# Two of the four high parts of the feed-forward's inner layer moved from VectorE to ScalarE, and the last group's z turned by TensorE

## The reference

```python
tgt1 = _layer_norm(tgt, g1, be1)
tgt = tgt + _self_attn(tgt1, mask, Wq, bq, Wk, bk, Wv, bv, Wo, bo)
tgt = tgt + (memory @ Wg.T + bg)
tgt1 = _layer_norm(tgt, g2, be2)
ff = jax.nn.relu(tgt1 @ W1.T + b1) @ W2.T + b2
return tgt + ff
```

## Time and profile before

| | us |
|---|---|
| median of three runs (lowest, highest) | 1756.54 (1755.94, 1760.69) |
| the profiled execution, its own time | 1759.22 |
| span of its trace | 1757.3 |
| mean granted clock of TensorE, as a share | 0.99 |
| busy: PE, DVE, ACT, POOL | 1684.2, 1509.3, 1393.1, 953.5 |

### The profile page before, as it was taken

One profiled execution on the slowest core, in us unless ns is written; L12 is line 12 of the kernel. 1 busy time (PEld: TensorE's weight loads), 2 busy tenths in 40 slices (PEclk: granted clock), 3 DMA queues, 4 the chain that ended last, 5 costly groups with the idle time before them and its releaser, 6 DMA issues. The chain is left out here.

```text
span 1757.3 us, 53486 instructions
## 1 busy us (share of the span) xinstructions
PE 1684.2 (96%) x17272; PEld 1643.0 (93%) x17272; DVE 1509.3 (86%) x7136; ACT 1393.1 (79%) x5506; POOL 953.5 (54%) x906
## 2 busy tenths in 40 slices
PE   6799999999999999999999999999999999999997
PEld 5699999999999999999999999999999999999997
DVE  7798898898888888888888888888888888888873
ACT  4788788788788788788788788788788787787782
POOL 5355545545545545555555555555555555555544
PEclk8899999999999999999999999999999999999999
DMA  5434444444444444444444444444444444444421
GB/s 187 130 124 138 140 131 138 131 139 132 134 142 130 137 140 130 136 141 131 136 145 128 136 142 131 135 142 132 134 139 136 133 141 135 128 146 135 128 91 37
DMA packets 258951, 233.77 MB, mean 133 GB/s; under 512 B 26992, under 2 KB 209136, under 8 KB 258672
## 3 DMA queue, kind: packets, MB, share of 16 engines
q1 hardware_dynamic: 258672, 230.35, 41.5%
HBM read 62.73 MB, written 16.78 MB: 45 GB/s over the span
## 5 line engine op out<-in xcount | busy, mean ns | idle before, releaser
L448 ACT ACTIVATE scores<-scores,row_min 128x128 f32<-128x128 f32 x2048 | 799.5, 406 | 37.1 <-DVE row_min L725 37.1
L874 POOL TENSOR_TENSOR hT_lo<-hid,hT_hi 128x512 fp32r<-128x512 f32 x256 | 339.6, 1327 | 687.7 <-DVE hT_hi L684 687.7
L725 DVE CUSTOM_DVE_ANT_0 scores<-score_ps,mask_bias 128x128 f32<-128x128 f32 x2048 | 467.8, 286 | 1.5 <-issue 1.1
L448 ACT ACTIVATION_READ_ACCUMULATOR scores<-scores,row_min 128x1 f32 x2048 | 420.5, 205 | 0.0
L460 ACT ACTIVATE probs<-turn_ps 128x512 f32<-128x512 f32 x512 | 306.3, 599 | 92.6 <-PE turn_ps L1022 92.6
L956 PE MATMUL ffn_ps<-w_hi,hT_lo 128*128 128x256 f32 x1024 | 301.2, 294 | 32.6 <-POOL hT_lo L874 32.2
L1022 PE MATMUL turn_ps<-ident,scores 128*128 128x128 f32 x2048 | 307.1, 273 | 5.3 <-ACT probs L460 5.3
L956 PE MATMUL ffn_ps<-zT_hi,w_lo 128*128 128x256 f32 x992 | 294.0, 296 | 1.4 <-ACT hid L501 1.2
L958 PE MATMUL ffn_ps<-w_hi,hT_hi 128*128 128x256 f32 x1024 | 284.2, 277 | 0.0
L957 PE MATMUL ffn_ps<-w_lo,hT_hi 128*128 128x256 f32 x1024 | 283.5, 277 | 0.0
L957 PE MATMUL ffn_ps<-zT_lo,w_hi 128*128 128x256 f32 x992 | 276.1, 278 | 0.0
(11 more groups left out here) (144 smaller groups left out, 4288.0 us busy)
## 6 DMA issues: line engine op xcount, KB each, us to landing
q_stack<-q_hi SPq DMA_DIRECT2D x128, 256.0 KB, 2.4
k_stack<-k_hi SPq DMA_DIRECT2D x256, 128.0 KB, 2.3
x_in<-x_dram SPq DMA_DIRECT2D x64, 256.0 KB, 2.7
mem_in<-memory_dram SPq DMA_DIRECT2D x64, 256.0 KB, 3.0
x_res<-x_dram SPq DMA_DIRECT2D x64, 256.0 KB, 3.0
q_stack<-q_lo SPq DMA_DIRECT2D x64, 256.0 KB, 2.3
k_stack<-k_lo SPq DMA_DIRECT2D x128, 128.0 KB, 2.3
inv<-inv_cols SPq DMA_DIRECT2D x256, 64.0 KB, 2.4
```

The costliest lines, as they stand in the source:

```text
L448: last = act.activation(exps, exps, ACT.Exp, bias=row_min[:, k, h:h + 1], scale=-1.0, accum_out=row_sum[:, k, h:h + 1])
L725: last = dve.tensor_tensor_reduce(out=scores[:, slot(i, t), h, :], in0=score_ps[t % 2][:, h * S:(h + 1) * S], in1=mask_bias[:, b, :], scal ...
L874: pool.tensor_tensor(halves[1], src, halves[0], ALU.subtract).then_inc(done, 1)
```

## The change

ACT now makes the high parts of the third and the fourth pair: right behind the two relu instructions of pair 2, and of pair 3, it waits for them and copies `hid` to `hT_hi`. DVE keeps the first two pairs. The new semaphore `hid_late_hi` tells POOL of the two that ACT makes, so each of the two semaphores counts two a group. In stage 64, for the last group only, DVE's turning in blocks and SP's four copies are gone: PE turns `xhat` with four transposes into a PSUM bank ahead of part 3 of the product with W2, ACT takes z's high part from that bank, and DVE the low part.

```diff
@@ ScalarE
                         last.then_inc(hid_relu, 1)
+                        if n >= 2:
+                            act.wait_ge(hid_relu, HJ * g + n + 1)
+                            act.activation(hT[0][:, 2 * n:2 * n + 2, :], hid[:, n % 2], ACT.Copy
+                                           ).then_inc(hid_late_hi, 1)
...
-                    if out_ and t == 12:
+                    if is_at(i, GROUPS) and t == 12:
+                        split_high(by_tile[1], zT[0][:], z_turned, 1, hid_ready, HJ * (GROUPS - 1), z_hi)
+                    elif out_ and t == 12:
@@ VectorE
-                    if ffn and t == 0:
+                    if is_at(i, GROUPS + 1) and t == 0:
+                        split_low(by_tile[1], zT, z_hi, GROUPS, z_split)
+                    elif ffn and t == 0:
...
-                    if ffn and t in HIDDEN_TICKS and t < 8:
+                    if ffn and t in HIDDEN_TICKS[:2]:
                         hidden_high(i - 2, HIDDEN_TICKS.index(t))
...
-                        dve.wait_ge(attnT_split, g + 1)
-                        turn_quads(attn_blocks, xhat2, ln2_ready, g + 1, z_blocked)
-                    if ffn and t == HIDDEN_TICKS[-1]:
-                        hidden_high(i - 2, HJ - 1)
+                        if i < GROUPS:
+                            dve.wait_ge(attnT_split, g + 1)
+                            turn_quads(attn_blocks, xhat2, ln2_ready, g + 1, z_blocked)
@@ GpSimd
-                        split_low(hid[:, n % 2], [h[:, 2 * n:2 * n + 2, :] for h in hT], hid_hi,
-                                  HJ * g + n + 1, hid_split)
+                        split_low(hid[:, n % 2], [h[:, 2 * n:2 * n + 2, :] for h in hT],
+                                  hid_hi if n < 2 else hid_late_hi, 2 * g + n % 2 + 1, hid_split)
@@ TensorE
+                    if is_at(i, GROUPS) and t == 12:
+                        pe.wait_ge(ln2_ready, GROUPS)
+                        pe.wait_ge(resid_ready, GROUPS)
+                        turn(by_tile[1], xhat2).then_inc(z_turned, 1)
@@ SyncE
-                if out_:
+                if out_ and i < GROUPS:
                     sp.wait_ge(z_blocked, i)
```

More of the change, by code:

```diff
@@ L226, in xattn_block @@
             sem(f"ln2_{n}") for n in ("stats", "mean", "var", "rstd", "ready"))
+        z_turned = sem("z_turned")
         z_blocked, z_cols, z_hi, z_split = (sem(f"z_{n}") for n in ("blocked", "cols", "hi", "split"))
         hid_ready, hid_relu, hid_hi, hid_split = (sem(f"s_hid_{n}") for n in ("ready", "relu", "hi", "split"))
+        hid_late_hi = sem("s_hid_late_hi")
         down_ready, resid_biased, y_summed = sem("down_ready"), sem("resid_biased"), sem("y_summed")
```

## The result

Before: 1757.43 us median (1755.94 to 1760.69, four runs; the 1756.54 of the table above was the median of three of them). After: **1823.55 us** (1806.31 to 1830.59, four runs). The recorded ratio, which weighs all runs, is 1.036, with a 95% interval of 1.028 to 1.044 (the two medians alone give 1.038): slower, and within the predicted 1762 to 1842 us, 6 us above the 1817.5. The profiled execution took 1826.82 us, with a span of 1825.0.

The account below looks back on a forecast made before the run. PE was taken to set the pace, 96% busy, with a second chain through DVE's norm and `values_of` almost as long. 1756.5 + 64 (61 stages at + 1.05) - 3 (last group) = 1817.5 us; range 1762 to 1842.

Parts of the forecast that it names:

- The sum of a stage: Per stage: DVE's chain + 1.86 - 0.27 us, less 0.54 slack, gives + 1.05 us; + 64 us over 61 stages.
- the slack of 0.54: Between ACT's copy of the probabilities and PE's `values_of`: 0.54 us a stage, beyond which delays lengthen the stage one for one.
- the two turns: POOL's low part of pair 3, then `xT_hi`, stop DVE's second norm, delaying it 1.86 us; chance 0.48.
- The loop: DVE's second norm and turning, z's copies, ACT's probabilities, PE's `values_of` and next fourth score matmul, back to DVE: 25.83 us.
- the first rival: Only one POOL instruction stops the second norm: + 0.21 us a stage, 1767 us, or 1773 with small delays; chance 0.27.
- some 1.5 us: PE's new wait each stage for ACT's copy of the probabilities ahead of `values_of`, replacing its wait for `hT_lo`.
- ACT's copies at nothing: ACT's two added copies, 1.4 us a stage, fall into its idle times and cost nothing; bounds 0 and 0.7 us.
- DVE's cast at 0.27: Removing DVE's cast at 813.07, ahead of the second norm, shortens DVE's chain by 0.27 us a stage.
- the last group at 3 us: Turning z on PE starts its product 2 us earlier and may avoid a 1.3 us clock loss: - 3 us once.
- Faster: the port doesn't matter: POOL's low part of pair 3 doesn't stop the second norm; 30 us gained, 1726 us; chance 0.15.
- PE's clock falls: PE's clock drops behind about 1.5 us idle each stage, adding 1.3 us a stage, about 1900 us; chance 0.03.
- The wait for `hT_lo`: PE's wait for POOL's low part: at most 32.2 us over 61 stages to gain, leaving PE alone at 25.84 a stage.

Follow-up runs that it names:

- 2: The changed kernel, with POOL's `xT_hi` also waiting until DVE has ended the second norm: 1782.80 us, ratio to before 1.012 to 1.015.
- 8: The changed kernel with only pair 3's high part on ACT, pair 2's back on DVE: 1842.49 us, ratio to before 1.047 to 1.051.
- 7: The changed kernel with only pair 2's high part on ACT, pair 3's back on DVE: 1738.04 us, ratio to before 0.986 to 0.989.
- 1: The changed kernel, with POOL's low part of pair 3 also waiting until the second norm has ended: 1724.55 us, ratio to before 0.979 to 0.982.
- 3: The kernel before, plus two unread copies of `hid` on ACT behind the relus of pairs 2 and 3: 1758.18 us, ratio 0.999 to 1.001.
- 4: The kernel before with only the last group's z turned by PE, as in the change: 1755.79 us, ratio 0.997 to 0.999.
- 9: The changed kernel, with POOL's low parts of pairs 1 and 3 waiting for the first and second norm: 1706.04 us, ratio to before 0.968 to 0.971.
- 10: The kernel before, with only POOL's low part of pair 1 waiting until the first norm has ended: 1712.17 us, ratio 0.972 to 0.975.
- 5: The kernel before, plus one unread addition on DVE ahead of the second norm: 1780.86 us, ratio 1.010 to 1.014.
- 12: The kernel before, with pair 3's cast to `hT_hi` and two unread DVE additions between second norm and turning: 1819.12 us, ratio 1.032 to 1.036.

## Why the prediction was right

**The sum of a stage.** "Chain: + 1.86 - 0.27" and "less the slack of 0.54: + 1.05 us" forecast a stage of 26.37 + 1.05 = 27.42 us; 27.42 and 27.44 stand in the trace. The norm's delay came out at 1.73 (2.61 - 0.88) and not 1.86, since the two turns follow each other closer than I had them, and 0.14 us came on top: 25.83 - 0.27 + 1.73 is 27.29, and the stage is 27.43. 2 and 8 show the same 0.14 and 0.17 us (8 without the - 0.27), so it isn't chance. The traces tell what it is. The loop is 25.88 by medians and not 25.83 (0.05), in part because PE follows the copy of `probs` by 0.10 us and not by the 0.06 that I took from another pair of engines. And DVE's way from `attn` to the norm is shorter by 0.21 and not by 0.27 (0.06). The last 0.03 is within what medians of parts leave over. The second of these is the small delay "of ACT's `k_hi`" that the first rival named with "up to 0.1 a stage". ACT's `k_hi` and DVE's `k_lo`, which waits for it, in a stage of the kernel before and in one of the kernel after:

```profile
805.36 0.84 ACT L515 ACTIVATE k_hi<-work_ps,qk_bias 128x256 fp32r<-128x256 f32 x2
806.68 0.84 DVE L788 SCALAR_TENSOR_TENSOR k_lo<-work_ps,qk_bias,k_hi 128x256 fp32r<-128x256 f32 x2
```

```profile
998.95 0.86 ACT L521 ACTIVATE k_hi<-work_ps,qk_bias 128x256 fp32r<-128x256 f32 x2
999.84 0.88 DVE L798 SCALAR_TENSOR_TENSOR k_lo<-work_ps,qk_bias,k_hi 128x256 fp32r<-128x256 f32 x2
```

Before, `k_hi` had ended 0.48 us before `k_lo` began (806.20 to 806.68); after, 0.03 (999.81 to 999.84), in most stages. For once the loop sets the pace, `values_of` starts 0.10 us behind ACT's copy where it started 0.62 behind, so ACT's program runs half a microsecond later beside PE's: `k_hi` starts 7.86 us behind the start of `values_of` in place of 7.34. In 7, where the loop doesn't set the pace, the same way of DVE is shorter by 0.32 us, so the cast was worth a little more than its 0.27, and the wait for `k_hi` costs about 0.1. In 1 the sum doesn't apply, since in most of its stages `values_of` doesn't wait for the copy. That the sum of a stage is right to 0.01 us is luck: the turns were 0.13 too long, and the rest 0.14 was missing. Its mechanism, the two turns and the loop, is what the traces show.

Of PE's wait I said "some 1.5 us" ahead of `values_of`. It is 1.09 in the median stage; the other part of PE's idle time stands in waits like the one for `hid` on the weight loads, 23.9 us in all.

**Two turns against one.** I gave 0.48 and 0.27, for "tenths". Both happen: two turns in about fifty stages, one in eleven. The first condition, POOL starting ahead of DVE, holds in both; the second, `xT_hi` ready in time, fails in the eleven. The Trainium skill ("SBUF — State Buffer", section "Who interferes with whom") has the rule for one turn, and the trace of 2 agrees, with 1.82 us in place of 0.88. What makes the loss of 66 us out of 25 is the second turn, which is beyond the rule.

**ACT's copies at nothing, DVE's cast at 0.27, the last group at 3 us.** Shown by 3 (0 us), by 8 against after (0.30 a stage), and by 4 (3.0 us, between 1.6 and 4.6 by its interval). In the last group the idle time goes from 1.23 + 2.74 to 1.38 us, the transposes take 0.60, so about 2 us are left as I had them, and the clock doesn't fall behind the 1.38. The 1.3 us for the clock are not safe: in the trace of 4 it fell a little earlier, as said above.

**The rivals.** "Faster: the port doesn't matter" fell at its own condition: the norm isn't left alone. But its mechanism stands: 1 fulfils the condition by a wait, and gives 1724.55 where the rival said 1726. "PE's clock falls" was put as all or nothing. It happens in four stages, in which a late landing has lengthened the wait to 1.96 to 2.44 us, less than the 2.74 on which the rival was built.

**The terms that were off.**
- *The wait for `hT_lo`.* I took 32.2 us / 61 = 0.53 from the rows of the matmuls, so PE alone at 25.84. It is 25.60 in 9 and 10, where nothing stops it: the wait cost 0.80 a stage. The row that shows it was in the same view, on the weight loads:

```profile
PEld ffn_ps L956 <- POOL hT_lo L874: 46.6, 61, 1.4
```

  46.6 / 61 = 0.76. The wait stood on the loads, and the matmul's own idle time leaves out the load that follows the wait. It left the sum as it is, since PE's own stage didn't decide, but it made the gain that was to be had look two thirds as large as it is (32.2 us, where 61 x 0.80 is 49), and the two limits look equal, where PE's is 25.60 and the loop's 25.88.
- *Late landings* had no term. Before, one landing is late, by 1.31 us (5.35 in place of 4.04), and its stage is 0.77 longer than 26.40: 1.31 less the slack of 0.54, to the hundredth. After the change the loop *is* the stage and there is no slack left: eight landings late by 0.85 to 1.6 us come through, with the clock in four: 15 us. The profiled execution took 1826.82 us, 6.8 above its forecast of 1820. Late landings and clock, less the 7.8 of the stages with one turn, are 7 to 8 us and account for that; the small delays beside them and the 3 us that the kernel before has of the same kind nearly cancel.
- *Where the slack applies.* "Whatever lengthens the part from the second norm to the turning by more than the 0.54 makes every stage longer" is true of the changed kernel. In the one before, 5 shows that a delay of 0.34 already costs 0.35, through `hT_lo`. The change removes this path as it adds its delay, so the step held for what it was used for.

## What to carry to other kernels

When an operation is moved to a free engine so that its result comes earlier, look at who consumes the result, and when it will now run: here POOL became free to start at the one moment at which DVE's critical instruction with two SBUF inputs starts. A wait that holds the uncritical engine back for the length of that instruction cost nothing here (POOL is busy for 54% of the span) and is worth trying on the kernel as it stands. And read the cost of a wait of PE from its weight loads as well as from its matmuls.

## What the runs showed of the hardware

- A DVE pair with two SBUF inputs that starts 0.15 us behind a POOL instruction stands for the whole of it, and once more for the next if that one is ready: 0.88, 1.82 and 2.61 us with none, one and two. A transposing instruction in the same place isn't slowed (1.16 to 1.19 us).
- The order isn't strict: with a POOL instruction waiting 0.16 us behind the start of a pair of additions, DVE kept its turn for both in 48 of the 64 pairs of 12 and lost it between the two in 15. What decides is open.
- Four small copies, from the issue of the first to ACT's start, take 4.04 us; 4.9 to 5.9 in 8 of 63 stages of the kernel after, of 2 and of 12, and in none to four of each of the others. Why the slow kernels have more of them is open.
- PE's granted clock fell to 0.53 in mid-program too. In the kernel after it fell behind idle times of 1.96, 2.11, 2.17 and 2.44 us and not behind 2.12, 2.35 and 2.66, so the length of the idle time alone doesn't decide (in the last group it fell behind 1.97 in 4 and not behind 1.55 before, nor behind 1.41 after the change); behind the 1.1 us of an ordinary stage it never did.
